# Linear attention and FFN on one core: from seven-product query-key blocks to seven-product up-projection over a whole batch

## The reference

```
kv  = sum over tokens of k^T v        (16 x 16 per head)
out = q kv ; out @ proj_w + proj_b
```

## Time and profile before

| | before |
|---|---|
| median of runs | 551.12 us |
| span of the profiled execution (its device time is not given apart) | 549.6 us |
| PE busy | 544.7 us, 2824 matmuls |
| DVE / ACT / POOL busy | 437.9 / 313.2 / 189.1 us |
| granted TensorE clock | full in all 40 slices |

### The profile page before, as it was taken

The page is one execution under the profiler, slowest core; times in us unless marked ns, Lnnn a source line. Parts: engine busy times, 40 slices in busy tenths (PEclk is TensorE's granted clock), DMA queues, the critical chain, the costliest instruction groups (busy, mean ns, idle before and its releaser), DMA issues.

```text
span 549.6 us, 9448 instructions
## 1 busy us (share of the span) xinstructions
PE 544.7 (99%) x2824; PEld 465.4 (85%) x2824; DVE 437.9 (80%) x856; ACT 313.2 (57%) x594; POOL 189.1 (34%) x196
## 2 busy tenths in 40 slices
PE   9999999999999999999999999999999999999997
PEld 7888788888888888888888888888888888888896
DVE  6977889688796987969788697987879778794846
ACT  4785734665537665474754656647565574734521
POOL 4242587320272312623235232543126340280010
PEclk9999999999999999999999999999999999999999
DMA  8422134352233424134251342524324242141723
GB/s 273 165 77 48 38 84 92 84 107 73 63 69 85 100 72 101 33 84 100 72 103 31 87 99 70 95 39 110 75 71 87 43 100 48 36 79 21 149 62 78
DMA packets 141415, 45.37 MB, mean 83 GB/s; under 512 B 133330, under 2 KB 136402, under 8 KB 141396
## 3 DMA queue, kind: packets, MB, share of 16 engines
q1 hardware_dynamic: 139280, 44.61, 35.1%
q10 hardware_dynamic: 2116, 0.53, 0.5%
HBM read 20.98 MB, written 8.39 MB: 53 GB/s over the span
## 4 chain that ended last, share of the span: by engine, by line
PE 91%; SPq 4%; ACT 3%; DVE 1%; issue 1%; DMA 0%; ACTq 0%
PE o_bank L1453 11%; PE o_bank L1454 11%; PE o_bank L1455 11%; PE w_bank L1453 10%; PE w_bank L1454 10%; PE w_bank L1455 10%; PE v_bank L1453 6%; PE v_bank L1455 6%; PE v_bank L1454 6%; SPq L372 4%; PE kv_bank L1629 2%; PE g_bank L1629 2%; PE kv_bank L1634 1%; PE g_bank L1634 1%; PE kv_bank L1647 1%; PE w_bank L1685 1%
## 5 line engine op out<-in xcount | busy, mean ns | idle before, releaser
L719 ACT ACTIVATE h_hi<-w_bank 128x512 fp32r<-128x512 f32 x128 | 75.6, 596 | 50.1 <-PE w_bank L1455 50.1
L1453 PE MATMUL w_bank<-xT_hi,w_hi 128*128 128x512 f32 x254 | 100.2, 394 | 0.2 <-DVE h_lo L1159 0.2
L1454 PE MATMUL w_bank<-xT_lo,w_hi 128*128 128x512 f32 x254 | 99.5, 392 | 0.0
L1455 PE MATMUL w_bank<-xT_hi,w_lo 128*128 128x512 f32 x254 | 98.9, 390 | 0.0
L1159 DVE SCALAR_TENSOR_TENSOR h_lo<-w_bank,h_hi 128x512 fp32r<-128x512 f32 x128 | 85.9, 680 | 15.2 <-ACT h_hi L719 13.5
L438 POOL TENSOR_TENSOR xn_lo<-xn,xn_hi 128x256 fp32r<-128x256 f32 x56 | 41.9, 748 | 151.2 <-ACT xn_hi L598 147.0
L1453 PE MATMUL o_bank<-h_hi,w_hi 128*128 128x512 f32 x240 | 93.8, 391 | 0.0
L1454 PE MATMUL o_bank<-h_lo,w_hi 128*128 128x512 f32 x240 | 93.8, 391 | 0.0
L1455 PE MATMUL o_bank<-h_hi,w_lo 128*128 128x512 f32 x240 | 93.4, 389 | 0.0
L486 POOL TENSOR_TENSOR y_sb<-y_sb,y_rows 128x256 f32<-128x256 f32 x56 | 62.9, 1127 | 9.4 <-DVE y_rows L1203 5.3
L1453 PEld LDWEIGHTS w_bank<-xT_hi,w_hi 128*128 128x128 f32 x254 | 47.9, 188 | 10.3 <-DVE h_lo L1159 1.9
(11 more groups left out here) (246 smaller groups left out, 1267.8 us busy)
## 6 DMA issues: line engine op xcount, KB each, us to landing
y_rows<-blocks SPq DMA_DIRECT2D x256, 32.0 KB, 1.9
x_sb<-x SPq DMA_DIRECT2D x15, 512.0 KB, 3.3
y_sb<-x SPq DMA_DIRECT2D x60, 128.0 KB, 3.1
out<-y_sb SPq DMA_DIRECT2D x58, 128.0 KB, 2.5
xT_raw<-blocks SPq DMA_DIRECT2D x224, 32.0 KB, 1.9
y_sb<-w SPq DMA_DIRECT2D x4, 256.0 KB, 5.4
x_sb<-x SPq DMA_DIRECT2D x2, 256.0 KB, 3.1
w_raw<-w SPq DMA_DIRECT2D x2, 256.0 KB, 7.1
```

The costliest lines, as they stand in the source:

```text
L719: nc.scalar.activation(h_hi[:, j % RING, :], w_bank[j % 2][:], ACT.Relu).then_inc(h_done, 1)
L1453: nc.tensor.matmul(to, left[0], right[0], start=first, stop=False, skip_group_check=shared)
L1454: nc.tensor.matmul(to, left[0], right[1], start=False, stop=False, skip_group_check=shared)
L1455: return nc.tensor.matmul(to, left[1], right[0], start=False, stop=last, skip_group_check=shared)
```

## The change

The seven-product form leaves query and key and goes to the up-projection. The left operand blocks are the W1 chunks: channels split in two (k = 0, 1), inner chunks in pairs, so a batch has four units n = 0..3 of two chunks; the right ones are the two halves of the batch. Each unit has 7 products of 3 matmuls of 512 columns and gives four outputs `UP_11, UP_12, UP_21, UP_22` (chunk pair row, half). It begins with batch 1; batch 0 keeps `ffn_up`.

- Query and key of all halves are made by `query_key` in whole tiles, into g_bank and kv_bank from batch 1 on.
- Both w banks hold one unit: up_a, up_b. The sum that had no bank is in SBUF (`up_fifth`).
- Output banks are o_bank for the first half and v_bank for the second; attention adds into the same banks (`add_attention` is gone), and runs at the head of the next batch.
- x_sb and y_sb hold one half instead of two, xn_hi and xn_lo too; xT_raw holds two.
- Four forms of W1 are made in the second half on GpSimd, and four sums of x blocks a batch (512 columns each).
- One loop body is one batch, with a new order on every engine. The extracts below are shortened to the calls and what they wait for.

```diff
-            def qk_begin ... qk_second ... qk_third ... qk_fourth
+            def up_fifth_product(b, n):
+                if n: wait(pe, up_lo_done[UP_21], unit(b, n) - 1)
+                else: wait(pe, xf_lo_done[X12_X11], b)
+                product(up_b, w1_form(S_ONE, n), x_form(X12_X11), True, False)      # -> up_fifth_in
+            def up_first(b, n):
+                ... wait(pe, up_lo_done[UP_12], unit(b, n) - 1)
+                product(up_a, w1_block(0, n, 0), x_block(0, 0), True, False)        # -> up_first_in
+            def up_second(b, n):  wait up_seeded;    up_a += W11 part               # -> up_11_in
+            def up_sixth(b, n):   wait up_seeded;    up_b += S_TWO x X22_T1         # -> up_sixth_in
+            def up_third(b, n):   wait up_12_seeded; up_a += S_FOUR x x_block(1, 1) # -> up_12_in
+            def up_seventh(b, n): wait up_12_seeded; up_b += W21 x X22_X12          # -> up_seventh_in
+            def up_fourth(b, n):  wait up_22_summed; up_b += W22 x X21_T2           # -> up_21_in
+            # ScalarE
+            def up_fifth_out(b, n): ... copy(up_fifth[:], up_b[:])
+            def up_seed(b, n):      ... copy(up_b[:], up_a[:])                       # -> up_seeded
+            def up_high(b, n, q):   relu into h_hi; for UP_22 a relu in place, then a copy
+            # VectorE
+            def up_seed_12(b, n):   up_a = up_b + up_fifth                           # -> up_12_seeded
+            def up_sum_22(b, n):    up_fifth = up_b + up_fifth                       # -> up_22_summed
+            def up_low(b, n, q):    as h_low, for UP_11, UP_12, UP_21
+            # GpSimd
+            def up_low_22(b, n):    h_lo[UP_22] = up_fifth - h_hi[UP_22]
```

The new second half, per engine:

```diff
 PE     ffn_up(1,1,2)  down 0  down 1  ffn_up 3  4  5  down 2  3  4  ffn_up 6  down 5  ffn_up 7
        gather(1,0,1)  down 6  key_value(0)  project(0)  down 7            (no query_key(2), no ffn_up(2))
 ACT    xn_high(1,1) h_high 3 ln_root(3) h_high 4 normalise(3,1) qT_high(0,0) h_high 5 6 k_high(1,1) h_high 7
        xT_high(1,1,0) xn_high(2,0) g_high(0) xT_high(1,1,1) m_high(0) qT_high(1,1) x_form_high x4
 DVE    variance(3) spread(3) h_low 3 transpose_x(3,1) divide(0,1,q) h_low 4 5 k_low(1,1) h_low 6
        transpose_q(1,1) xT_low(1,1,0) qT_low(0,0) g_low(0) h_low 7 mask_kv(0) xT_low(1,1,1) m_low(0)
        qT_low(1,1) x_form_low x4
 SP     move_x(3,0,1)  move_q(1,1)  load_y(0,0)
 POOL   split_xn(1,1)  weight_forms(0)  weight_forms(1)  x_form x2  weight_form_over  x_form x2  split_xn(2,0)
```

The loop body begins and ends so (PE), with the SyncE list beside it:

```diff
+ attend(b-1,0) up_first(b,0) up_fifth_product(b,0) query_key(s,0,0) query_key(s,0,1) up_sixth(b,0) up_second(b,0)
+ query_key x2  attend(b-1,1) up_seventh(b,0) up_third(b,0) query_key(s+1,1,0) up_fourth(b,0) down(b,0,UP_11)
...
+ up_seventh(b,3) up_third(b,3) down(b,3,UP_11) up_fourth(b,3) down(b,3,UP_12) down(b,3,UP_21) down(b,3,UP_22)
+ SP: load_x(s+3) move_x(s+2) store_y(b-1,0) move_q(s,0) load_y(b-1,1) move_x(s+3) store_y(b-1,1)
+     move_q(s+1,1) load_x(s+4) load_y(b,0)
```

More of the change, by code:

```diff
@@ L391, in _ @@
             sp.dma_start(bias_ffn[:], b2.partition_broadcast(P)).then_inc(bias_o_loaded, 16)
-            load_x(3, 1)
+            load_x(3, 1, 2)
             def opening():
-                load_x(4, 0)
-                move_x(2)
+                load_x(4, 0, 3)
+                move_x(2, 0, 0)
                 move_q(0, 0)
[L399 to L413, removed]
@@ L415, in end, with second_half @@
[L415 to L425 removed]
+            def second_half():
+                move_x(3, 0, 1)
+                move_q(1, 1)
+                load_y(0, 0)
@@ L846, in second_half @@
[L846 to L873 removed]
+                ln_root(3)
@@ new lines, in batch @@
+            def batch(b, s):
+                variance(s + 2, b + 1, 0)
+                spread_y(b - 1, 0, 0)
+                sum_squares(s, 0)
+                up_low(b, 0, UP_11)
+                sum_squares(s, 1)
+                spread(s + 2)
+                up_seed_12(b, 0)
+                spread_y(b - 1, 0, 1)
+                sum_squares(s, 2)
+                sum_squares(s, 3)
+                bound(s)
+                up_sum_22(b, 0)
+                norms(s)
+                transpose_x(s + 2, 0)
@@ new lines, in batch @@
+                k_low(s, 0)
+                up_sum_22(b, 1)
+                sum_squares(s + 1, 2)
+                sum_squares(s + 1, 3)
+                bound(s + 1)
+                up_low(b, 1, UP_12)
+                norms(s + 1)
+                divide(1, 1, k_done)
+                spread_y(b - 1, 1, 1)
+                spread(s + 3)
+                up_low(b, 1, UP_21)
+                k_low(s + 1, 1)
+                transpose_x(s + 3, 1)
+                g_low(b)
+                up_low(b, 2, UP_11)
@@ new lines, in batch @@
+                up_seed_12(b, 2)
+                divide(0, 1, q_done)
+                up_sum_22(b, 2)
+                up_low(b, 2, UP_12)
+                up_low(b, 2, UP_21)
+                transpose_q(s + 1, 1)
+                mask_kv(b)
+                up_low(b, 3, UP_11)
+                up_seed_12(b, 3)
+                qT_low(s, 0)
+                up_sum_22(b, 3)
+                up_low(b, 3, UP_12)
+                m_low(b)
+                up_low(b, 3, UP_21)
+                xT_low(b + 1, 0, 0)
@@ L1443, in end @@
+                up_low(b, 3, UP_12)
+                up_low(b, 3, UP_21)
+                m_low(b)
+                qT_low(s + 1, 1)
+            def end(b):
                 for k in range(KC):
-                    spread_y(b, 1, k)
-            all_batches(dve, opening, half, end)
+                    spread_y(b, 0, k)
+                add_rows(b)
+                add_last(b)
+            all_batches(dve, opening, second_half, batch, last_batch, end)
         @block.tensor
```

1377 lines of the change are left out of this document (687 added, 690 removed).

## The result

The changed kernel takes 569.12 us (median of 4 runs, 568.73 to 570.75) against 551.41 for the kernel before on the same chip (551.05 to 551.78): a ratio of 1.0326, 95% interval 1.0311 to 1.0341. The forecast was 555.0, range 548.8 to 563.0: slower was right, the size was not, and the range does not hold it. The profiled execution has a span of 567.6 us; the median stands 1.5 above it, as the forecast took it.

A forecast was written before the change was run, and what follows sets the result against it. PE was taken as the bound, busy 544.7 of 549.6 us. 549.6 - 12.7 (work) + 12 (opening) + 3.6 (loop) + 0.9 (end) = 553.4 of span; with 1.5 to the median 554.9, said as 555.0, range 548.8 to 563.0.

The forecast's parts named there:

- PE's work: Matmul time on PE: -12.7 us, from -19.2 in the up-projection and +6.5 in query and key; a turn 64.8.
- the steps listed for `g_low`: Second half, after half 3's move lands at 73.1: DVE's steps to the end of `g_low`, 78.4, where key_value can start.
- the second road: Second half: `move_q(1,1)` after `move_x(3)`, then x forms, put `up_fifth_product(1,0)` at 86.2, batch 1 at 82.7: 10.1 lost.
- Opening: Second half, before batch 1: +12 us (bounds +10.1 to +13.5) from PE's holes while it waits for other engines.
- the named transpose: Second half: `transpose_x` of half 3, from which both chains to batch 1 start, forecast to end at 61.5.
- The clock rival: Holes before batch 1 make PE's clock fall to 1.2 GHz: +2 to +5 us, 557 to 560; chance 0.1.
- Loop, +0.6 a turn: Each loop turn loses 0.6 us to late helper steps, within 0 to 1.5; +3.6 us in all.
- None is a bound: Loop: the changed loads of DVE, ACT and POOL, with POOL gaining 4 x 1.3 us, were judged not to limit a turn.
- The ring through SyncE: Loop: SyncE's moves and dependent steps sum to 64.7 against PE's 64.8; as rival 6 to 13 us, 557.5 to 564.5, chance 0.2.
- My sign for it: Loop: turns above 66 with PE's waits at `up_seed` and SyncE never idle before `move_x`.
- The other side: Rival of a cheap start at +10.1 and a loop without holes: 548.5 us; chance 0.15.
- Last batch: Last batch and end: +0.9 us, 0.5 for one late step and 0.4 for a wider last add and store; bounds 0 to 2.

The follow-up runs named there:

- the cut split: The changed kernel with GpSimd's split of xn in the loop cut to 8 of 256 columns: 563.16 us, ratio 1.0210.
- both cuts: The changed kernel with GpSimd's split of xn and add_rows in the loop both cut to 8 of 256 columns: 561.33 us.

## Why the prediction was wrong

- **PE's work**: right in kind, 3 us too small in size. Back to back a turn is 64.3, not 64.8. It never showed, as PE was not back to back.
- **Sums**: the steps listed for `g_low` add up to 78.1, not 78.4, those to attend from there to 84.5, not 85.1 (+11.9 instead of +12.5), and those of the second road to 86.7, not 86.2. None of this moves the forecast of +12 by more than its rounding.
- **Opening**, the first step that failed. Its roads and waits came as written, at the named places, and moving the named transpose moved batch 1 by 3.8. Mis-sized was DVE's part before the transpose, which I priced by the earlier trace rows, where GpSimd rested: 61.5 forecast, 63.7 found. The rest of the miss is from key_value on: 9.65 us to batch 1 where I had 6.7, of which the clock makes 2.3. Filling the holes gains 1.0 us net, and leaving out the forms' sums 2.75.
- **The clock rival**: it came true (0.50 in two spells, chance given 0.1), at 2.3 us from key_value on, the low end of its 2 to 5, and 1.0 net. The first spell lay ahead of a later wait: PE still waited 3.1 us for `g_low` behind it.
- **Loop, +0.6 a turn**: the step that cost most. The term is 2.4 over 64.3. I named `up_seed(b, 3)`, `k_low` and `up_low(b, 3, UP_21)` as narrow, and said that "each of these can cost a step of 0.6, so 0 to 1.5 a turn"; I took the average as if they did so rarely. They cost 0.26, 0.65 (0.5 where PE has waited just before) and 0.32, and they do so in every turn. `up_low(b, 1, UP_21)`, 0.77 in four turns of six, I had not named. Priced wrongly was GpSimd: its busy time goes from 189.1 to 226.8 and a split instruction takes 948 ns in the mean; I put that down as "None is a bound", when a job of 4.3 us lies on the chain with the least cover.
- **The ring through SyncE**: argued as the cause of the 0.6 and as a rival; the run with the stores moved gives it nothing in the steady loop. My sign for it, that SyncE is never idle before `move_x`, was wrong by my own sum, which leaves SyncE 64.7 - 48.2 = 16.5 us without an issue. The sum itself was not far off: `qT_high` waits for the landing in each turn once turns are at 65.4 and 65.1. So the ring lies close behind, within about 1 us of PE's own 64.3, and it took 0.7 us of PE in turn 2 of the changed kernel.
- **The other side** (548.5): its conditions were an opening of +10 or less and a dense loop. Even with batch 1 at 79.64 (7.0 over dense) the loop, at 67.1 a turn in the mean and so 2.8 over dense, keeps the time at 561.
- **Last batch**: +0.9 forecast, 0.7 more than that found; no run looks at this term.

That most of the loop's lost time comes from GpSimd's jobs is shown by the cut split (-6.0 us) and both cuts (-7.8). How the split's effect divides between slower DVE steps and the late `normalise` stays open. That turns differ is in part a matter of which waits PE meets: the turns of 66.8 and 67.38 have the gap of 0.77 before the fifth product of unit 2, two of the three of 66.4 don't, and the one of 67.38 also has the gap of turn 2. Why PE meets it in one turn and not in the next stays open.

## What to carry to other kernels

A kernel whose bounding engine has no hole spends all of its savings in holes if the new order makes the helpers late by even tenths at places met in each turn; count the cover of each due step with the helpers at the lengths that they have beside each other, not at their free ones. An engine with 40% busy time is not free when one of its jobs lies beside a chain with 0.3 us of slack. Removing one limit can bring up one that lay just behind it, here the ring. And swapping neighbours by hand mostly moves a hole: take away the shared cause first.

## What the hardware did that I had not expected

- Four values a partition cost VectorE 1.89 us beside a GpSimd sum of 2.34 us (0.17 alone); with four GpSimd instructions in a row, small steps took 0.57 to 0.74 for 0.16, one such wait each. What a step loses is not set by its own size but by what is left of the GpSimd instruction that it meets: `ln_v` ended 0.03 us after the sum. The Trainium skill (SBUF - State Buffer, Who interferes with whom) says that whoever comes first holds the shared pair for its whole instruction; the trace agrees.
- The same one-input step, `ln_v`, was held by a GpSimd `memset` too (0.48 us, to 0.03 after its end), while a two-input step beside the next `memset` was not (0.16).
- PE loses tenths that its list of waits does not show: before `down(b, 3, UP_21)` the starts are 0.32 us late in each turn (0.21, and 0.11 at the next matmul), before `up_second(b, 3)` 0.26, and the list names neither. A wait that it does name costs 0.16 more than it says, as counted above, and 0.1 at the next matmul.
